# Causal attention of eight cores: key blocks taken in pairs, and the last stage's PSUM copies given to ScalarE

## What is computed

```python
xn = _layernorm(x)
# attention: 16 heads of 128, causal
q = xn @ w_dq.T @ w_uq.T
kv = xn @ w_dkv.T @ w_ukv.T
k, v = jnp.split(kv, 2, axis=-1)
attn = jnp.einsum('bhqd,bhkd->bhqk', q, k) * SCALE
attn = softmax(attn + mask)              # mask: -inf above the diagonal
out = jnp.einsum('bhqk,bhkd->bhqd', attn, v) @ w_out.T
# FFN with ternary weights and activations rounded to 127 steps
h = _silu(_bitlinear(xn, w_gate)) * _bitlinear(xn, w_up)
return x + out + _bitlinear(h, w_down)
```

## Time and profile before

| what | us |
|---|---|
| runs of the kernel before (3): median | 5495.9 |
| lowest and highest of them | 5443.53 and 5555.84 |
| profiled execution, its own time | 5414.32 |
| span of its slowest core (core 4) | 5412.8 |
| spans of the eight cores | 5362.2 to 5412.8 |

### The profile page before, as it was taken

One profiled execution on the slowest core, in us unless ns is written; L12 is line 12 of the kernel. 1 busy time (PEld: TensorE's weight loads), 2 busy tenths in 40 slices (PEclk: granted clock), 3 DMA queues, 4 the chain that ended last, 5 costly groups with the idle time before them and its releaser, 6 DMA issues.

```text
span 5412.8 us, 44659 instructions; the slowest of 8 cores (5362.2 to 5412.8 us)
## 1 busy us (share of the span) xinstructions
PE 3403.8 (63%) x13124; PEld 1249.4 (23%) x13124; DVE 2345.6 (43%) x3102; ACT 882.8 (16%) x886; POOL 155.1 (3%) x245
## 2 busy tenths in 40 slices
PE   2434431476666566566656657688888887359992
PEld 1111110122121111111111112233333333124442
DVE  3444444323351514334151422655555552666554
ACT  2333333123112020111202010000000001210000
POOL 0000000101000000000000000000000000000000
PEclk9556655698675666767666569899999998569996
DMA  4333311677220202022020204645554442445544
GB/s 137 109 114 104 104 68 68 184 227 260 86 89 15 104 1 103 25 79 73 31 103 1 87 25 126 209 141 154 156 156 156 147 133 84 149 122 152 145 128 155
DMA packets 344783, 610.03 MB, mean 113 GB/s; under 512 B 10530, under 2 KB 228130, under 8 KB 306978
## 3 DMA queue, kind: packets, MB, share of 16 engines
q1 hardware_dynamic: 303634, 348.74, 21.1%
q0 software_dynamic: 40720, 255.87, 14.0%
HBM read 554.24 MB, written 50.33 MB: 112 GB/s over the span
## 4 chain that ended last, share of the span: by engine, by line
PE 51%; DVE 20%; issue 15%; DMA 6%; ACT 6%; DVEq 1%; PEldq 0%; SPq 0%; ACTq 0%; POOL 0%; POOLq 0%
PE psp L1028 7%; PE psb L888 4%; PE psp L710 4%; PE psp L607 4%; PE psp L888 4%; PE psb L646 4%; PE psb L904 4%; PE psp L904 4%; PE psb L650 4%; DVE accTw L404 4%; ACT xntb L340 2%; DVE hqfm L974 2%; DMA pe<-wuT 2%; PE psb L435 2%; DVE hstg L871 2%
## 5 line engine op out<-in xcount | busy, mean ns | idle before, releaser
L1028 PE MATMUL psp<-hqfm,tdq 128*128 128x512 bf16 x2048 | 454.5, 380 | 25.0 <-PE psp L1028 17.7
L634 DVE TENSOR_TENSOR ptile<-ptile,masksb 128x512 bf16<-128x512 bf16 x64 | 27.2, 426 | 870.5 <-ACT ptile L614 870.5
L357 PE MATMUL psp<-identb,xntb 128*128 128x128 bf16 x352 | 93.4, 265 | 489.2 <-ACT xntb L340 288.7
L614 ACT ACTIVATE ptile<-psp 128x1024 bf16<-128x1024 f32 x288 | 294.9, 1024 | 592.5 <-PE psp L607 591.4
L607 PE MATMUL psp<-qfm,kg 128*128 128x512 bf16 x576 | 229.0, 489 | 230.3 <-issue 159.2
L710 PE MATMUL psp<-wukv,ckv 128*128 128x256 bf16 x1152 | 284.4, 399 | 105.6 <-PE psp L710 66.0
L888 PE MATMUL psp<-tgq,xqfm 128*128 128x512 bf16 x1024 | 301.3, 404 | 63.4 <-DVE hstg L871 53.9
L888 PE MATMUL psb<-tgq,xqfm 128*128 128x512 bf16 x1024 | 299.1, 408 | 53.3 <-DVE hstg L871 32.4
L904 PE MATMUL psb<-tuq,xqfm 128*128 128x512 bf16 x1024 | 273.2, 379 | 27.6 <-ACT hg L894 15.3
L646 PE MATMUL psb<-ptile,onesb 128*64 128x512 bf16 x576 | 220.1, 472 | 96.5 <-PE psp L607 66.6
L904 PE MATMUL psp<-tuq,xqfm 128*128 128x512 bf16 x1024 | 271.2, 379 | 10.7 <-ACT hg L894 0.9
(11 more groups left out here) (158 smaller groups left out, 4070.4 us busy)
## 6 DMA issues: line engine op xcount, KB each, us to landing
xt<-wdT POOLq DMA_DIRECT2D x64, 1024.0 KB, 5.1
gsq<-wgT SPq DMA_DIRECT2D x64, 1024.0 KB, 7.4
usq<-wuT SPq DMA_DIRECT2D x64, 1024.0 KB, 7.7
dslab<-wdT SPq DMA_DIRECT2D x128, 512.0 KB, 4.1
xt<-wuT POOLq DMA_DIRECT2D x40, 1024.0 KB, 6.1
pa<-wgT POOLq DMA_DIRECT2D x36, 1024.0 KB, 6.2
xt<-xk SPq DMA_DIRECT2D x36, 1024.0 KB, 5.6
hs<-hstg POOLq DMA_DIRECT2D x16, 2048.0 KB, 9.4
```

Source lines behind the costliest of these rows:

```text
L614: a = S.activation(out=ptile[:, pb, :, :].rearrange("p h c -> p (h c)"), in_=bank2(sp), func=AF.Exp, scale=SCALE, bias=EXPB)
L1028: mm = T.matmul(out=bank(bp + nh), lhsT=tdq[:, hcc, :], rhs=hqfm[:, hcc, nh * 512:(nh + 1) * 512], start=(hcc == 0), stop=(hcc == 63))
```

## The change

It has two parts. In the sweep, key blocks are taken in pairs: after scores(0) and scores(1), each round waits for the second exponential of the pair (and the masks of both), gives PE the post matmuls of both blocks, and then the scores of the next two. The scores of the pair behind a boundary are given to PE ahead of that boundary. In the last stage, the four copies out of PSUM go from VectorE to ScalarE, in the same order and sizes, and VectorE's additions wait for the fourth.

```diff
             emit_scores(0)
-            for j in range(NKC):
-                half = 0 if j < nA else 1
-                pb = (j - jlo) % 2
-                if j + 1 < NKC and j + 1 != nA:
-                    emit_scores(j + 1)
...
-                    wt(T, "mV", pvm)
-                else:
-                    wt(T, "mS", exp_sm[j])
+            emit_scores(1)
+            for jb in range(0, NKC, 2):
+                j0, j1 = jb, jb + 1
+                half = 0 if j0 < nA else 1
+                pvm = 0
+                for j in (j0, j1):
...
+                wt(T, "mS", exp_sm[j1])
+                if pvm:
                     wt(T, "mV", pvm)
-                if fin_vm and j == nA:
+                if fin_vm and j0 == nA:
                     wt(T, "mV", fin_vm)
...
+                for j in (j0, j1):
...
+                    post_tm[j] = inc(mm, T)
+                if jb + 2 < NKC:
+                    emit_scores(jb + 2)
+                    emit_scores(jb + 3)
+                if j1 == half_last[half]:
                     fin_vm = boundary(half)
                     nb += 1
-                    if j + 1 < NKC and j + 1 == nA:
-                        emit_scores(j + 1)
...
-            wt(V, "mT", tm)
+            ys = ystg[:, tb % 2, :]
+            wt(S, "mT", tm)
+            if tb >= 2:
+                wt(S, "g0" if tb % 2 == 0 else "g1", y_dg[tb - 2])
+            inc(S.activation(out=ys[:, 0:512], in_=psb0[:], func=AF.Copy), S)
+            inc(S.activation(out=ys[:, 512:1024], in_=psb1[:], func=AF.Copy), S)
+            inc(S.activation(out=ys[:, 1024:1536], in_=psb6[:], func=AF.Copy), S)
+            sm4 = inc(S.activation(out=ys[:, 1536:2048], in_=psb7[:], func=AF.Copy), S)
+            wt(V, "mS", sm4)
             wt(V, "x0" if tb % 2 == 0 else "x1", dd)
-            if tb >= 2:
-                wt(V, "g0" if tb % 2 == 0 else "g1", y_dg[tb - 2])
-            ys = ystg[:, tb % 2, :]
-            inc(V.tensor_copy(out=ys[:, 0:512], in_=psb0[:]), V)
...
```

More of the change, by code:

```diff
@@ new lines, in emit_attn_sweep @@
+            for jb in range(0, NKC, 2):
[3 more added lines that the diff above has]
+                for j in (j0, j1):
+                    mp = (j - (nA - 4)) if j < nA else (j - 32)
+                    if 0 <= mp < 4:
+                        nmask += 1
+                        pb = (j - jlo) % 2
+                        wt(V, "mS", exp_sm[j])
+                        inc(V.tensor_tensor(out=ptile[:, pb, 0, :], in0=ptile[:, pb, 0, :],
+                                            in1=masksb[:, mp, :], op=ALU.mult), V)
+                        pvm = inc(V.tensor_tensor(out=ptile[:, pb, 1, :], in0=ptile[:, pb, 1, :],
+                                                  in1=masksb[:, mp, :], op=ALU.mult), V)
+                wt(T, "mS", exp_sm[j1])
+                if pvm:
@@ L638, in emit_attn_sweep @@
                     wt(T, "mV", pvm)
-                else:
-                    wt(T, "mS", exp_sm[j])
-                if fin_vm and j == nA:
+                if fin_vm and j0 == nA:
                     wt(T, "mV", fin_vm)
[L643 to L653, removed]
+                for j in (j0, j1):
+                    pb = (j - jlo) % 2
+                    st = (j == half_first[half])
+                    sp_ = (j == half_last[half])
+                    for hh in range(HPG):
+                        T.matmul(out=(psb6 if hh == 0 else psb7)[0:64, :],
+                                 lhsT=onesb[:, 0:64], rhs=ptile[:, pb, hh, :],
+                                 start=st, stop=sp_)
+                    for hh in range(HPG):
+                        mm = T.matmul(out=bank(hh), lhsT=vg[:, j - jlo, hh * 128:(hh + 1) * 128],
+                                      rhs=ptile[:, pb, hh, :], start=st, stop=sp_)
+                    post_tm[j] = inc(mm, T)
@@ L1064, in emit @@
             tm = inc(tm_, T)
-            wt(V, "mT", tm)
-            wt(V, "x0" if tb % 2 == 0 else "x1", dd)
-            if tb >= 2:
-                wt(V, "g0" if tb % 2 == 0 else "g1", y_dg[tb - 2])
-            ys = ystg[:, tb % 2, :]
-            inc(V.tensor_copy(out=ys[:, 0:512], in_=psb0[:]), V)
-            inc(V.tensor_copy(out=ys[:, 512:1024], in_=psb1[:]), V)
-            inc(V.tensor_copy(out=ys[:, 1024:1536], in_=psb6[:]), V)
-            inc(V.tensor_copy(out=ys[:, 1536:2048], in_=psb7[:]), V)
+            ys = ystg[:, tb % 2, :]
[7 more added lines that the diff above has]
+            wt(V, "mS", sm4)
+            wt(V, "x0" if tb % 2 == 0 else "x1", dd)
             inc(V.scalar_tensor_tensor(out=ys[:, 0:1024], in0=psp23[:],
```

## The result

| | before | after |
|---|---|---|
| median of 10 runs each, us | 5474.39 | 5815.83 |
| profiled execution: span of the slowest core | 5412.8 (core 4) | 5794.2 (core 7) |
| sweeps, mean over 8 cores and 8 groups, us | 125.9 | 166.6 |
| the same, times 8 | 1007 | 1333 |
| last stage, mean over the cores, us | 103.2 | 99.6 |

A forecast was written before the change was run, and what follows sets the result against it. PE was taken to set the pace of the steady sweep loop. Sweeps +199 us and last stage +3 us made +202 us on a median of 5495.9 us: 5698 us, range 5580 to 5870 us.

The forecast's parts named there:

- Rounds at either clock: Sweep loop: a two-block round takes 5.87 us against 4.46 at full clock, 8.01 against 7.04 at half clock.
- Masks, opening, boundary: Per sweep: four masked pairs +4.2 us, opening +1.2 us, boundary +1.0 us at full clock or +1.4 at half.
- The clock: Sweeps keep the old half-and-half mixture of clock levels: 153.7 us each, +24.9 us a sweep, +199 us in eight.
- my own sign: Sweep timeline: forecast wrong if rounds are not 5.87 and 8.01 us, or the share of the two levels moves.
- The two ends: A changed sweep all at full clock, 136.0 us, or all at half clock, 177.3 us; +58 or +388 us in eight.
- Rival 1: PE keeps 2.4 GHz in the sweeps: +58 + 3, 5557 us, 1.1% slower; chance 0.11.
- Rival 2: PE falls to 1.2 GHz for all of the sweeps: +388 + 3, 5887 us; chance 0.17.
- Rival 3: In sweeps ScalarE does not stand in PE's way; only opening and masks cost: 5540 us; chance 0.02.
- Keys, values, FFN: Stages outside the sweeps and last stage: claimed unchanged.
- Code branched past: Stands ahead of sweeps, 159.2 us: fewer PE waits in the code might save 0 to 12 us; taken as 0.
- The last stage: Four PSUM copies per block on ScalarE take 3.40 us plus hand-over, against 3.18 on VectorE: +3 us.

The follow-up runs named there:

- the two filled kernels: Unread matmuls added in the sweep: five per round in the changed kernel, 1.0225 of the time before; one behind each scores burst in the kernel before, 0.9817.
- the late wait one block at a time: Kernel before, its order kept, but posts of each block also wait for the next block's exponential: 1.0612 of the time before.

## Why the prediction came out as it did

The direction, the place and the mechanism were right: slower, in the sweeps, because PE stands for the second exponential. The forecast was 5698 us, +202; measured were 5815.83 us, 341 more than the 5474.39 of the kernel before. The sweeps' growth of 326 us is what the forecast had as +199. Point by point:

- **Rounds at either clock.** 5.87 and 8.01 us were worked out; rounds wholly at one level take 5.8 and 8.0 us. PE's stand was to be 1.65 and 1.23 us, it is 1.70 and 1.32. Right.
- **Masks, opening, boundary.** With the rounds they made +27.5 us a sweep at full clock; the two filled kernels differ by 25.8 us. Close. The masks' part shows in the timeline: a masked round's stand is 2.76 us, 1.06 more than 1.70, where I had 1.05. The waits for masks ahead of the posts are 82.9 us on core 4, for which I had 8 × 4.2 = 34 us: they hold the part of the stand that an unmasked round has too.
- **The clock.** Here is the term that was mis-sized. I kept the old sweeps' half and half. By the same scale (136.0 us a sweep at full clock, 177.3 at half clock) the measured 166.6 us stand at 74% of the way. This puts a sweep 0.31 × 41.3 = 12.9 us above the forecast's 153.7 us, 103 us in eight, most of the missing 127 us; the remainder is that the old sweeps' mean over all cores (125.9) lies 3 us below that of core 4 from which I started. By my own sign ("or if the share of the two levels moves") this part was wrong: the time at 1.2 GHz went from 55% to 75%. The step that failed is the sentence "I take what is nearest, the old sweeps' own mixture". Its rows showed a loop that kept 2.4 GHz with no stand over 0.26 us. I carried this over to a loop that stands 1.7 us in each round, though I had written down that longer stands speak for the lower level. What the runs show in its place: with the late wait and the pairs together the level falls 453 times in plain rounds, where it fell in none before. That stands alone would decide it is no better a rule: with the late wait one block at a time, PE stands for a larger part of each step (1.32 of 3.3 us), and there the old mixture nearly stayed (61% of the time at 1.2 GHz against 55%).
- **One block is not at one clock.** The two ends assumed whole rounds at either level. Of 1,088 rounds on the eight cores some 50 take 5.8 us and some 280 take 8.0 us; 457 lie between. The timeline shows rounds with scores at 0.59 and posts at 1.03 us: the dear part, eight of twelve matmuls, is what comes right behind the stand.
- **Rival 1, the clock held by long bursts,** fell. The Trainium skill's rule that long stands between bursts bring the clock down (TensorE: Matmul & The Clock Gate, "Why this matters for your kernels") agrees with the boundaries, where PE stands for 7 us and all 118 falls of the kernel before lie; that only long stands do, as I had used it, this case does not bear out: 453 falls lie in rounds that stand for 1.7 us. The same page's section on brief stands between groups of matmuls ("A second HAM failure mode: psum-queue depth-cycling") describes such swings between the levels; that the mixture would stay by it was my conclusion, and it shifted. Rival 2, all at half clock, was too dark: behind the stand the clock comes up again, ten times a sweep, 508 of the 645 times under a matmul of line 648, the posts' second half.
- **Rival 3, ScalarE not in the way,** fell: 172.5 us of waits. But in the run in which each block waits for its own exponential, in the same order, 50.3 us of such waits are left on core 4: over two thirds of it was avoidable.
- **Keys, values, FFN** unchanged but for the stretches named above: from the keys' first matmul to their last the mean grew by 283 us, and the seven sweeps between make 285. **Code branched past:** the stand ahead of the sweeps' first matmuls was 159.2 us and is of the same order, 168.2 us "issue" ahead of line 607 on core 4; nothing there speaks against taking 0.
- **The last stage.** +3 us forecast, -3.6 us measured. ScalarE's copy takes 0.60 us and the next starts 0.69 us after it; I had taken a Silu's 0.69 us as its length and 0.16 us for the gap, which is 0.09. The estimate of 613 ns from the Trainium skill (ScalarE: Activation LUTs, "What ACT_TABLE_LOAD costs") was within 3% of the 597 ns measured; with the gap of 0.16 us it still gave the wrong sign for the stage. No table load appeared.

## What to carry to other kernels

When a change makes TensorE wait, price the wait at both clock levels, and take the mixture between them for a term of its own that the old loop does not give: here it moved by 20 points with 1.7 us once in 5.8, and by 6 with 1.3 us once in 3.3. Until a trace shows the new pattern, the two ends are the honest range, and counting the falls of the clock by place in a trace tells which stands matter. A wait belongs ahead of the instruction that needs it, not ahead of a group of them. And where the granted clock is a mixture, a matmul that nobody reads, put where PE stands anyway, tells what the clock costs.

## What the runs showed of the hardware

- A stand of PE of 1.70 us in each round of 5.8 us (two blocks, posts behind each other) went with 453 falls of the granted clock to 1.2 GHz in the plain rounds of 64 sweeps. A stand of 1.32 us in each step of 3.3 us went with 7, and kept 2.4 GHz for the 38 us shown; stands of 0.25 us, two in 2.23 us, went with none.
- At the boundaries, where PE stands for 7 us, the clock fell in every kernel, also where the steps between were filled.
- One extra matmul in each step of the kernel before raised the mean clock of the sweeps from 0.73 to 0.84 and cost 0.02 us of a step.
- PE's matmul bursts that follow each other without waiting for their own ends make a step 0.7 us shorter (2.23 to 1.52 us), for the two ends that were waited for.
- ScalarE copies 512 columns of fp32 out of PSUM in 597 ns, VectorE in 692 ns.
